# z of units 2 to 6 in another PSUM bank, and the first units in another order

## What is computed

```python
att   = softmax(MLP(cond))                            # 8 weights for each of 64 batches
mixed = einsum(att, weight[8,64,64]) @ x + bias       # a 64x64 mix of each batch's rows
q, k, v = mixed @ Wq, mixed @ Wk, mixed @ Wv          # q (32 x 32 heads), k, v (32)
o     = softmax_e(q[d] * k[e] / sqrt(32)) @ v         # with heads summed as below
x     = x + broadcast(o)
h     = grouped_conv1d(x, 9 taps, 4 groups) + ctx(cond) + bias
x     = x + h @ dequant4bit(packed).T + bias
```

## Time and profile before

| | |
|---|---|
| timed runs, median | 435.32 us (434.19 to 435.57) |
| profiled execution | 433.03 us, span 430.9 us |
| TensorE busy | 412.5 us, 96% |
| VectorE busy | 365.2 us, 85% |
| GpSimd busy | 341.2 us, 79% |
| ScalarE busy | 224.5 us, 52% |
| DMA | 79.07 MB, mean 183 GB/s |

### The profile page before, as it was taken

The page is one execution under the profiler, slowest core; times in us unless marked ns, Lnnn a source line. Parts: engine busy times, 40 slices in busy tenths (PEclk is TensorE's granted clock), DMA queues, the critical chain, the costliest instruction groups (busy, mean ns, idle before and its releaser), DMA issues. The chain is left out here.

```text
span 430.9 us, 6747 instructions
## 1 busy us (share of the span) xinstructions
PE 412.5 (96%) x2185; PEld 347.8 (81%) x2185; DVE 365.2 (85%) x606; ACT 224.5 (52%) x464; POOL 341.2 (79%) x314
## 2 busy tenths in 40 slices
PE   4968989999999999999999999999999999999997
PEld 3967888888888888888888888888888888888785
DVE  2897899998979999899989799998989899983331
ACT  3846535636545274747456364737364556572700
POOL 4082529859696999999999979899988979899920
PEclk9969899999999999999999999999999999999999
DMA  8999457160736776665717282927285371818112
GB/s 328 368 367 348 192 133 287 34 191 10 215 118 206 247 187 234 183 237 152 270 33 289 92 265 81 303 107 204 118 206 213 77 242 32 293 19 255 50 53 97
DMA packets 52593, 79.07 MB, mean 183 GB/s; under 512 B 38464, under 2 KB 38592, under 8 KB 48192
## 3 DMA queue, kind: packets, MB, share of 16 engines
q1 hardware_dynamic: 51168, 77.08, 54.0%
q10 hardware_dynamic: 1376, 1.31, 1.0%
HBM read 61.11 MB, written 17.27 MB: 182 GB/s over the span
## 5 line engine op out<-in xcount | busy, mean ns | idle before, releaser
L1158 PE MATMUL p_f<-w_ffn,u_hi 128*128 128x512 f32 x512 | 196.0, 393 | 0.0
L1158 PE MATMUL p_f<-w_ffn,u_lo 128*128 128x512 f32 x512 | 194.7, 390 | 0.0
L600 ACT ACTIVATE u_sb<-p_conv,u_bias,cols_sb 128x128 f32<-128x128 f32 x256 | 94.9, 460 | 40.3 <-PE p_conv L1152 39.8
L1158 PEld LDWEIGHTS p_f<-w_ffn,u_lo 128*128 128x128 f32 x512 | 96.2, 188 | 20.4
L1158 PEld LDWEIGHTS p_f<-w_ffn,u_hi 128*128 128x128 f32 x512 | 96.2, 188 | 20.4
L449 POOL TENSOR_TENSOR c_lo<-xc,c_hi 128x516 fp32r<-128x516 f32 (+1 forms) x66 | 82.3, 1256 | 22.2 <-ACT c_hi L590 14.7
L460 POOL TENSOR_TENSOR xn<-xn,bias_n 128x1024 f32<-128x1024 f32 x32 | 76.7, 2418 | 3.2 <-DMA xn<-xn_in_in 3.2
L590 ACT ACTIVATE c_hi<-xc 128x516 fp32r<-128x516 f32 (+1 forms) x68 | 41.0, 609 | 68.4 <-POOL xc L441 66.4
L436 POOL TENSOR_TENSOR xc<-xc,o_c 128x384 f32<-128x384 f32 x60 | 54.5, 908 | 23.6 <-DMA o_c<-o_dram 22.4
L902 DVE TENSOR_TENSOR xn<-p_f,xn 128x512 f32<-128x512 f32 x64 | 43.4, 678 | 22.8 <-PE p_f L1158 22.4
L889 DVE STREAM_TRANSPOSE p_ut<-u_sb 128x512 f32<-128x512 f32 (+1 forms) x68 | 46.1, 683 | 18.2 <-ACT u_sb L600 18.2
(11 more groups left out here) (111 smaller groups left out, 456.9 us busy)
## 6 DMA issues: line engine op xcount, KB each, us to landing
xc<-xc_in_in SPq DMA_DIRECT2D x16, 1032.0 KB, 7.5
xn<-xn_in_in SPq DMA_DIRECT2D x16, 1024.0 KB, 8.8
out<-xn SPq DMA_DIRECT2D x31, 512.0 KB, 4.8
xt<-xt_in_in SPq DMA_DIRECT2D x15, 1024.0 KB, 5.6
o_c<-o_dram SPq DMA_DIRECT2D x116, 32.0 KB, 2.7
xn<-wq_in SPq DMA_DIRECT2D x4, 512.0 KB, 11.9
xt<-wq_in SPq DMA_DIRECT2D x1, 1024.0 KB, 5.9
xn<-wq_in SPq DMA_DIRECT2D x1, 1024.0 KB, 7.9
```

The costliest lines, as they stand in the source:

```text
L600: ins = eng.activation(u_sb[:, g % 2, i * P:(i + 1) * P], p_conv[g % 2][:, i * P:(i + 1) * P], ACT.Identity, bias=u_bias[:, g, bat:bat + 1 ...
L1158: return mm(p_f[half][:, :], u[:, (k // TU) % 2, r, t * P:(t + 1) * P], w_ffn[:, r, 512 * half:512 * half + 512], **flags)
```

## The change

Three kinds of edit. z of units 2 to 6 is made in `p_f[1]` (before: 2 and 3 only). The waits follow: `project(3)` to `project(6)` each wait for the copy of the z before theirs, and no longer for o or adds; `mix(2)` waits for its own z and the last `add_first`, `mix(3)` and later no longer for all seven early z; `open_bank(0, 1)` waits for all seven. And the lists of calls of units 0 to 4 are put in another order on all five engines. No call is added or removed. The loops are the same. The program:

```diff
 def z_ps(a):
-    if a in (2, 3):
+    if 2 <= a < NZ:
         return p_f[1][:, 0:TU * W3]
-    if a in (5, 6):
-        return p_sm[1][:, TU * W3:2 * TU * W3]
-    return p_sm[a % 2 if a < NZ else (Z_AT[a] + 3) % 2][:, TU * W3:2 * TU * W3]
+    return p_sm[1 if a < NZ else (Z_AT[a] + 3) % 2][:, TU * W3:2 * TU * W3]
 def z_before(a):
-    return max([a + 1] + [NZ] * (a >= 3) + [v + 1 for v in Z_AT if Z_AT[v] <= a - 3])
+    return max([a + 1] + [v + 1 for v in Z_AT if Z_AT[v] <= a - 3])
 def project(a, t, half=None):
...
-    if a in (3, 6):
+    if 3 <= a < NZ:
         eng.wait_ge(s_zc, a)
-    if a == 4:
-        eng.wait_ge(s_add, TU * G)
-    if a in (4, 5):
-        eng.wait_ge(s_o, TU * (a - 3))
 def mix(a):
-    eng.wait_ge(s_zc, a + 1 if a < 2 else 5 if a == 2 else z_before(a))
+    eng.wait_ge(s_zc, z_before(a))
     if a >= 2:
         eng.wait_ge(s_o, TU * (a - 1))
+    if a == 2:
+        eng.wait_ge(s_add, TU * G)
 def open_bank(k, half):
...
     else:
-        eng.wait_ge(s_zc, 4)
+        eng.wait_ge(s_zc, NZ)
```

More of the change, by code:

```diff
@@ L980, in _ @@
             sum_exp(2, 0)
+            add_edges()
+            sum_exp(2, 1)
+            times_v(2, 0)
+            c_low(2, 0)
             u_low(1, 0)
-            c_low(2, 0)
+            times_v(2, 1)
             turn_u(1, 2)
-            times_v(2, 0)
-            u_low(1, 1)
             c_low(2, 1)
             sum_v(2, 0)
-            turn_u(1, 3)
             divide(2, 0)
-            sum_exp(2, 1)
-            u_low(1, 2)
-            finish(0, 0)
-            u_low(1, 3)
-            times_v(2, 1)
-            turn_u(2, 0)
             sum_v(2, 1)
             divide(2, 1)
+            u_low(1, 1)
+            u_low(1, 2)
+            turn_u(1, 3)
+            finish(0, 0)
+            turn_u(2, 0)
+            u_low(1, 3)
+            softmax_top(3)
+            finish(0, 1)
             turn_u(2, 1)
-            finish(0, 1)
+            score(3, 0)
             u_low(2, 0)
-            softmax_top(3)
-            score(3, 0)
+            score(3, 1)
+            subtract(3, 0)
+            u_low(2, 1)
             turn_u(2, 2)
-            u_low(2, 1)
+            turn_u(2, 3)
             finish(1, 0)
             u_low(2, 2)
-            turn_u(2, 3)
-            subtract(3, 0)
             u_low(2, 3)
-            score(3, 1)
             sum_exp(3, 0)
@@ L1020, in _ @@
             divide(3, 1)
+            finish(2, 0)
             turn_u(3, 0)
-            finish(2, 0)
+            softmax_top(4)
             turn_u(3, 1)
-            softmax_top(4)
             score(4, 0)
-            u_low(3, 0)
             finish(2, 1)
             score(4, 1)
+            u_low(3, 0)
             u_low(3, 1)
@@ L1271, in _ @@
             copy_o(0, 0)
-            mix(1)
+            project(2, 1, 0)
+            project(2, 1, 1)
             copy_o(0, 1)
-            project(2, 1, 1)
+            project(3, 0, 0)
             copy_o(0, 2)
+            project(3, 0, 1)
             conv(0, 0)
+            conv(0, 1)
+            project(3, 1, 0)
             copy_o(0, 3)
-            conv(0, 1)
+            project(3, 1, 1)
             copy_o(1, 0)
@@ L1294, in _ @@
             project(4, 1, 1)
+            mix(2)
+            conv(1, 0)
+            project(5, 0, 0)
+            conv(1, 1)
+            project(5, 0, 1)
+            linear(0, 0)
             conv(1, 2)
-            mix(2)
-            project(5, 0, 0)
-            project(5, 0, 1)
             project(5, 1, 0)
-            linear(0, 0)
+            mix(3)
+            project(5, 1, 1)
             linear(0, 1)
-            project(5, 1, 1)
+            conv(1, 3)
+            project(6, 0, 0)
+            project(6, 0, 1)
+            project(6, 1, 0)
+            project(6, 1, 1)
             linear(0, 2)
@@ L1306, in _ @@
             linear(0, 5)
-            project(6, 0, 0)
-            project(6, 0, 1)
-            conv(1, 3)
+            linear(0, 6)
+            linear(0, 7)
             conv(2, 0)
-            project(6, 1, 0)
-            linear(0, 6)
-            project(6, 1, 1)
-            linear(0, 7)
             conv(2, 1)
             conv(2, 2)
+            project(7, 0)
+            project(7, 1)
+            conv(2, 3)
             linear(1, 0)
-            mix(3)
-            conv(2, 3)
             linear(1, 1)
             linear(1, 2)
-            project(7, 0)
             linear(1, 3)
@@ L1325, in _ @@
             linear(1, 5)
+            mix(4)
             linear(1, 6)
-            project(7, 1)
             linear(1, 7)
-            mix(4)
+            conv(3, 0)
             linear(2, 0)
```

180 lines of the change are left out of this document (86 added, 94 removed).

## The result

The changed kernel takes 438.85 us (median; 433.88 to 441.39), the kernel before, timed beside it, 434.4 us (431.9 to 438.08). The ratio is 1.0081, with a 95% interval of 1.0055 to 1.0107: slower by 3.5 us, where 433.0 and a gain of 2.3 were forecast. (The two medians lie 4.45 us apart; where this text compares kernels it goes by the ratios, each with its own interval.) One of the 22 executions, that of 441.39 us, was in the slow state and is left out of the ratio. The profiled execution took 438.48 us with a span of 436.1 (before 433.03 and 430.9).

A forecast was written before the change was run, and what follows sets the result against it. TensorE was taken to bound the kernel from 62 us on, the order before that setting its start. Gross gain 3.6 less 1.3 for the clock gives 2.3: profiled 433.03 becomes 430.7, median 433.0 us; range 431.1 to 435.5.

The forecast's parts named there:

- What bounds the kernel: From 62 us on the kernel runs at TensorE's pace; the order before that decides when this steady part begins.
- The chain from the last `divide` to the conv: Save, spread, `add_o`, `c_low`, conv after a unit's last `divide`: 13.6 us to `conv(3, 0)`, 14.1 to `conv(4, 0)`.
- The bank edit, 0: z of units 2 to 6 in `p_f[1]`: removed waits had no idle time, added ones are covered; worth 0.
- rival (b): `z_copy(6)`, behind `c_high(2, 0)` and `add_edges`, holds `linear(0, 3)`: 2 to 3 us lost, 434.6; chance 0.22 with no effect.
- The first stall: TensorE's early gaps, idle at 24.6 to 26.2 and 2 us for z of unit 1, lie in VectorE's shadow.
- the cited rule: Trainium skill on TensorE's clock: the throttled state is the default and activity releases it.
- The clock, 1.3 us: TensorE's low clock near 34 to 37 and 51 to 54 us takes 1.3 us off the gain.
- rival (c): Low clock on the critical lines, slower from 9.8 us; two 6.8 us stretches make it 2.0 slower, 437.3; chance 0.11.
- VectorE's line, 3.8 us gained: Up to `divide(3, 1)`: 3.93 us of idle time goes, less 0.15, so that `divide` ends at 99.95 us.
- TensorE's line: From `copy_o(1, 3)` at 50.7 without a wait to `conv(3, 0)` at 90.2; `conv(4, 0)` at 114.2, against 117.82.
- `add_edges` at 2.95 us: VectorE's `add_edges`, ahead of `c_high(2, 0)` and `z_copy(6)`, taken at its 2.95 us from the kernel before.
- Queues, 0: Moved loads cost 0: `load_x(5)` earlier, `load_c(2)` behind `save_o(2, 1)`, `load_c(4)` behind two stores.

The follow-up runs named there:

- e8: e7 with `x_o(3)` ahead of `add_o(3, 0)`, `x_o(0)` and `x_o(1)` ahead of `c_low(1, 3)`, `z_copy(6)` ahead of `c_high(2, 0)`: 433.28 us, ratio 0.9995.
- e11: Kernel before with the bank edit and its waits, `project(4, 0, 0)` behind `project(3, 1, 1)`, `project(6)` ahead of `linear(0, 2)`: 438.43 us, ratio 1.0089.
- e4: Kernel before with 15 extra matmuls on unused data in TensorE's first gap, ahead of `project(2, 0, 0)`: 431.78 us, ratio 0.9958.
- e1: Changed kernel with 23 extra matmuls on data nobody reads, where TensorE stands idle early: 438.40 us, ratio 1.0094 to the kernel before.
- e6: e5 with the load of x of unit 3 ahead of the bias and xn of unit 0, two xc loads swapped: 435.96 us, ratio 1.0027.
- e7: e6 with the 23 filler matmuls of e1 in TensorE's early gaps: 433.76 us, ratio 1.0011 to the kernel before.
- e2: Changed kernel with `mix(1)` behind two halves of `project(2, 1)` and `project(2, 1, 1)` before `copy_o(0, 0)`, no work added: 437.62 us, ratio 1.0074.
- e9: e8 with `load_c(2)` back ahead of the saves of unit 2, as in the kernel before: 433.95 us, ratio 0.9996.
- e5: Changed kernel with `copy_o(0, 2)` put ahead of `project(3, 0, 0)`: 436.83 us, ratio 1.0054 to the kernel before.

## Why the prediction was wrong, step by step

- **What bounds the kernel** was right: the loss at `conv(4, 0)`, 5.68 us, is the loss at the end (5.2) to half a microsecond. The chain from the last `divide` to the conv was no worse than forecast: 14.07 us to `conv(3, 0)` and 13.5 to `conv(4, 0)`, forecast 13.6 and 14.1, with TensorE waiting at neither. In e8, where it does wait, it was 15.2, so it isn't a constant.
- **The bank edit, 0: wrong.** The step counted the copy's own 0.33 us and the work on TensorE beside it, but not what stands ahead of the copy on ScalarE. In the new order the waits before the projections are covered, as forecast, but `open_bank(0, 1)` now waits for the last copy, and that costs the 1.20 us at `linear(0, 3)`. It was named as rival (b), with "no margin", and then put at 0 in the sum. In the old order e11 prices the edit, with the moves it needs, at 1.0089, 3.9 us.
- **The first stall, "in VectorE's shadow": wrong, and with the next two steps the one that failed the forecast.** The gap at 24.9 was forecast at 1.6 us and is 1.84, that at `mix(1)` at 2 us and is 2.39. But the gaps cost through the clock behind them, and there VectorE is not a shadow: e4 fills the gap, the low clock goes, and VectorE's waits of 2.16 and 1.34 us go with it. The idle time that the new order was to remove was the price of the low clock, not of the order. The step on the clock adds that stalls made shorter give nothing back; that is its own inference and not the cited rule, and the traces don't bear it out as a rule: behind the 1.84 us at 24.9 the clock held.
- **The clock, 1.3 us: right in place and kind, wrong in size.** It falls at 33, where 34 was said. It lasts 17 us; the forecast took its lengths, 3.4 and 6.8 us, from the dips of the kernel before, and rival (c) set 9.8 us as the point from which it measures slower. That point was passed. The second stretch, behind 51 us, didn't come. The length was not one number to be forecast at all: by the mean clocks it differs from one execution to the next, and the time with it (433.88 us at 0.996, 438.67 to 439.70 at 0.972). No experiment takes the low clock away from the changed kernel and nothing else. The filler of e1 takes 10 of the 17 us and gives nothing, since x of unit 3 is not there; with `copy_o(0, 2)` and x repaired it goes with 0.7 us by the ratios and 2.2 by the medians (e6 to e7).
- **VectorE's line, 3.8 us gained: wrong.** All the idle time that went came back elsewhere, and more: 5.50 us of waits up to 50 us, of which 1.46 is one matmul group put behind a projection. Through `add_first(1, 1)` it reached **TensorE's line**, whose own work was forecast well (23.8 us between the convs, 23.93 measured) but which was to start from `copy_o(1, 3)` at 50.7 and started at 57.16. **Missed altogether:** that x of unit 3 is issued at 30.7 and lands at 40, after 9.3 us; where TensorE is faster, that becomes its next wait (2.31 us in e1, 3.52 in e2). The forecast followed x of unit 2 and not of unit 3. Missed too: `x_bias(2)` and `x_o(2)` ahead of `c_low(2, 2)`, 0.87 us of TensorE's time at `conv(2, 2)`; and `x_o(3)`, 1.42 us on VectorE, which turned out to lie beside the path. The diff moves them, the step on the queues mentions none of them.
- **`add_edges` at 2.95 us: mis-sized**, 4.21 us in the new order. In both kernels GpSimd works beside it; in the new one it is an addition to xn, which takes 2.72 us there, and with that moved away `add_edges` takes 3.08 (e8). Over all runs it is 4.14 to 4.21 us in the seven kernels with that addition beside it and 2.71 to 3.09 in the seven without. The Trainium skill (SBUF, section "Who interferes with whom") states that a VectorE instruction with two SBUF inputs contends with a GpSimd instruction that reads SBUF. `add_edges` has two such inputs, and 4.19 against 3.08 agrees; which GpSimd operations collide how strongly, no run here separates.
- **Queues, 0:** right for `load_c(2)` (e9).
- **Rivals.** (b) and (c) happened together, with mechanisms that were on no list: `copy_o(0, 2)` behind `project(3, 0, 0)`, and `c_low(2, 2)`. The chance of 0.11 for slower came from requiring two long low stretches; in the profiled execution one did it, longer than any in the trace of before, with two small waits of TensorE.

How the 3.5 us divide can't be read as a sum, because the causes hide each other. In the order in which they were taken away the ratio goes 1.0081, 1.0054 (`copy_o(0, 2)`), 1.0027 (the loads), 1.0011 (clock), 0.9995 (the small ones). Neighbouring steps overlap in their intervals, the ends don't, and neither do the kernel after and e6 (just), nor e1 and e7: the place of `copy_o(0, 2)` and of the loads, together, is shown as a cause by time. That the low clock is one in the changed kernel rests on how its executions differ, not on an edit. With everything mended the new order is level with the old one, whose own head is still unmended; with that mended too, the old one is at 0.9958. What still holds e8 back in its trace is TensorE's wait of 2.06 us at `conv(3, 0)`, as long as the 2.1 us by which the second save is slow. The save is not all of it: e6 waits 1.01 us at the same place with both saves at 1.4.

**Open:** why the second save lands in 3.1 to 3.5 us in six kernels and in 1.4 in the others. How much of the step from e5 to e6 is the loads and how much noise. And what decides whether the clock falls at a gap and how long it stays low, which differs between executions of one program.
